# A part kept in SBUF until the merge: when a PSUM bank comes free in a cross-network kernel on one core

## The chip, the cores and the metric

The kernel runs on one core of a Trainium2 chip. The time is that of the device for one execution, in microseconds; lower is better. The kernel before was run three times: median 1504.7 us (1504.6, 1504.7 and 1512.56).

## The reference

For each of 1024 rows, 39 embeddings of 16 numbers are fetched and go through three layers of products (a compressed interaction network), and the results through a small MLP:

```python
x0 = xk = inputs                      # (1024, 39, 16)
for W in (f0, f1, f2):                # W: (F*G, 128)
    z = einsum('bfd,bgd->bfgd', x0, xk).reshape(b, f * g, d)
    cur = einsum('bpd,pm->bmd', z, W) # (1024, 128, 16)
    outs.append(cur); xk = cur
result = sum(concatenate(outs, axis=1), axis=-1)      # (1024, 384)
h = concatenate([result, dense_ctx], axis=1)
h = maximum(h @ W_top1 + b_top1, 0); h = maximum(h @ W_top2 + b_top2, 0); y = h @ W_top3
```

All data is fp32.

## The kernel before

The rows are worked in 8 batch tiles of 128 rows. Each batch tile is four groups (q = 0 to 3), each group four tiles (j = 0 to 3) of 128 columns (8 rows by 16 dimensions). There are 128 tiles in all, numbered t.

The second layer (f1) is where the time goes. For each tile, TensorE multiplies the first layer's result cur0 with f1 for all 39 fields, four fields at a time: that is a **chunk**, c = 0 to 9, of 512 columns in one PSUM bank (chunk 9 has three fields, 384 columns). A chunk is three matmuls, since the product is split in high and low parts: L738, L739, L740. The 39 products of a tile are then each scaled by their field's x and summed. Two ways of doing this share the work:

- chunks 0 and 1, 4 and 5, 8 and 9 (units 0, 2, 4; a **unit** is two banks): ScalarE scales each field in place (L465), then VectorE adds the unit's eight fields in one reduce: L610 for unit 0 (step **R0**, it starts sum_a), L619 for unit 2 (step **R1**, it writes the **part**), L630 for unit 4 (step **R2**, it gives the tile's result, cur1).
- chunks 2, 3, 6 and 7: VectorE multiplies and adds field by field (L605; the first into sum_b is L596), alternately into sum_a and sum_b. These are the steps from FUSE2, FUSE3, FUSE6 and FUSE7 on.

After R1 the part is added to sum_a (L621, **JOIN**). The last but one field of chunk 7 leaves sum_b plus itself in its own bank (LAST_B). The **MERGE** (L627) adds sum_a to that and puts it into the free fourth slot of chunk 9's bank, where the last reduce takes it in.

Every engine runs its instructions in the order in which they are written; semaphores tie the engines together. VectorE counts its 21 steps a tile on the semaphore acc_steps. Y is a ring of three units, six banks: chunk c of a tile goes to the bank that was used three units earlier, and TensorE waits for the step in the table FREED that sets this bank free (L727 to L730). So chunk 9 goes where chunk 3 was, chunks 0 and 1 of the next tile where 4 and 5 were (R1), chunk 2 where 6 was, chunk 3 where 7 was (MERGE), chunk 4 where 8 was (R2).

Between the chunks TensorE has other matmuls at fixed places: the first layer's sums of the next group (L686, seven a group: before chunks 2, 5 and 8 of j=1, chunks 1, 4 and 7 of j=2, chunk 0 of j=3), the product that spreads a tile's cur1 (L694, before chunk 5), transposes of the next batch tile's rows (before chunk 2 where q=2), the transposes of the scalars (L673, before chunk 9 of j=3), the third layer of the batch tile before (L700, before chunks 0 to 3 of j=0 where q is 1 to 3), and the MLP (L708 to L724, in the first tile of q=0 from batch tile 2 on, and in tile 125). In j=3 VectorE also splits the next group's cur0 (L572) and sums it (L574) right before R1. GpSimd gathers the rows and multiplies the pairs for the first layer.

In batch tile 0 and in q=0 of batch tile 1 there is neither third layer nor MLP; these are called plain groups below.

Of the kernel before, what the change touches and what calls it, by code (L numbers as in the profile page):

```python
# [8 lines left out]
ALU = mybir.AluOpType  # L9
ACT = mybir.ActivationFunctionType  # L10
AX = mybir.AxisListType

P = 128
B, NF, D = 1024, 39, 16
M = 128
# [30 lines left out]
SUM_SLOT = 3  # L46


R0, FUSE2, FUSE3, R1, JOIN, FUSE6, FUSE7, MERGE, R2 = 1, 2, 6, 10, 11, 12, 16, 20, 21
NST = 21  # L50

LAST_B = (7, 2)
FREED = {0: R0, 1: R0, 2: FUSE2 + 3, 3: JOIN, 4: R1, 5: R1, 6: FUSE6 + 3, 7: MERGE, 8: R2, 9: R2}


SLOTS = JT * CH
# [75 lines left out]
def build(nc, dense, ids, tables, w1, b1, w2, b2, w3, f0, f1, f2, out):  # L132
    ctx = ExitStack()
    with ctx:
        def sb(name, shape, dt=F32):
            return ctx.enter_context(nc.sbuf_tensor(name, shape, dt))
# [4 lines left out]
        def sem(name):  # L141
            return ctx.enter_context(nc.semaphore(name))
# [26 lines left out]
        x_col = sb("x_col", [P, QG, JT, FC])  # L169
        sum_a = sb("sum_a", [P, 2, M])  # L170
        sum_b = sb("sum_b", [P, 2, M])
        cur1 = sb("cur1", [P, 2, M])

        x_block = sb("x_block", [P, 2, JT, TB * FC])
# [30 lines left out]
        y_filled, scaled, acc_steps = sem("y_filled"), sem("scaled"), sem("acc_steps")  # L205
# [29 lines left out]
        def bank(t, c):  # L235
            b = 2 * ((UNITS * t + c // 2) % UB) + c % 2
            return Y[:, 512 * b:512 * (b + 1)]

        def unit(t, u):
            b = 2 * ((UNITS * t + u) % UB)  # L240
            return Y[:, 512 * b:512 * (b + 2)].rearrange("p (s m) -> p m s", m=M)
# [287 lines left out]
        def _(dve):  # L529
# [40 lines left out]
            def split_cur0(g):  # L570
                dve.wait_ge(cur0_high_ready, g + 1)
                dve.tensor_tensor(cur0_low[:, g % 2, :], C[:], cur0_high[:, g % 2, :].bitcast(F32),  # L572
                                  ALU.subtract).then_inc(cur0_ready, 1)
                dve.tensor_reduce(z0[:, GB * g % (3 * P):GB * g % (3 * P) + GB],  # L574
                                  C[:].rearrange("p (b d) -> p b d", d=D), AX.X, ALU.add).then_inc(c_read, 1)

            def layer2_read(bt, part):
                z = z2[:]
                dve.wait_ge(l2_filled, L2_PARTS * bt + part + 1)
                if part == 0:  # L580
                    dve.tensor_copy(z, C[:, 0:P]).then_inc(c_read, 1)
                else:
                    dve.wait_ge(c_read, C_USE["l2", bt, part])
                    dve.tensor_tensor(z, C[:, 0:P], z, ALU.add).then_inc(c_read, 1)

            def fuse(t, c, first, starts):

                n0 = NST * t
                q, j = t // JT % QG, t % JT
                dve.wait_ge(y_filled, CH * t + c + 1)  # L590
                for i, f in enumerate(CH_F[c]):
                    acc = (sum_a, sum_b)[(i + starts) % 2][:, t % 2, :]
                    src = bank(t, c)[:, i * M:(i + 1) * M]
                    x = x_col[:, q, j, f:f + 1]
                    if c == 2 and i == 1:
                        dve.tensor_scalar(acc, src, x, None, ALU.mult).then_inc(acc_steps, 1)  # L596
                    else:
                        before = first + i - 2
                        if c == 2 and i == 0:
                            before = R0  # L600
                        if c == 6:
                            before = (FUSE3 + 3, JOIN)[i] if i < 2 else before
                        dve.wait_ge(acc_steps, n0 + before)
                        to = src if (c, i) == LAST_B else acc
                        dve.scalar_tensor_tensor(to, src, x, acc, ALU.mult, ALU.add).then_inc(acc_steps, 1)  # L605

            def tile(t, g, q, j):
                n0 = NST * t
                dve.wait_ge(scaled, NSC * t + 2)
                dve.tensor_reduce(sum_a[:, t % 2, :], unit(t, 0), AX.X, ALU.add).then_inc(acc_steps, 1)  # L610
                fuse(t, 2, FUSE2, 0)
                fuse(t, 3, FUSE3, 0)
                if j == 0 and q and g >= QG:
                    layer2_read(g // QG - 1, q - 1)
                if j == JT - 1 and g + 1 < NG:
                    split_cur0(g + 1)
                dve.wait_ge(scaled, NSC * t + 4)
                part = bank(t, 3)[:, 0:M]
                dve.tensor_reduce(part, unit(t, 2), AX.X, ALU.add).then_inc(acc_steps, 1)  # L619
                dve.wait_ge(acc_steps, n0 + R1)  # L620
                dve.tensor_tensor(sum_a[:, t % 2, :], part, sum_a[:, t % 2, :], ALU.add).then_inc(acc_steps, 1)  # L621
                fuse(t, 6, FUSE6, 1)
                fuse(t, 7, FUSE7, 1)
                dve.wait_ge(scaled, NSC * t + 6)
                dve.wait_ge(acc_steps, n0 + FUSE7 + 3)
                c, i = LAST_B
                dve.tensor_tensor(bank(t, 9)[:, SUM_SLOT * M:], bank(t, c)[:, i * M:(i + 1) * M], sum_a[:, t % 2, :],  # L627
                                  ALU.add).then_inc(acc_steps, 1)
                dve.wait_ge(acc_steps, n0 + MERGE)
                dve.tensor_reduce(cur1[:, t % 2, :], unit(t, 4), AX.X, ALU.add).then_inc(acc_steps, 1)  # L630

            split_cur0(0)
            for g in range(NG):
                for j in range(JT):
                    tile(JT * g + j, g, g % QG, j)
# [4 lines left out]
        def _(pe):  # L640
# [86 lines left out]
            def chunk(t, c):  # L727
                v = UNITS * t + c // 2 - UB
                if v >= 0 and (c % 2 == 0 or v % UNITS not in SCALED_UNITS):
                    pe.wait_ge(acc_steps, NST * (v // UNITS) + FREED[2 * (v % UNITS) + c % 2])  # L730
                g, j = divmod(t, JT)
# [121 lines left out]
```

## Time and profile before

| | |
|---|---|
| median of 3 runs | 1504.7 us |
| the profiled execution | 1519.59 us |
| its span | 1517.5 us |
| TensorE matmul busy (PE) | 1363.7 us, 90% |
| VectorE busy (DVE) | 1140.5 us, 75% |
| ScalarE busy (ACT) | 912.2 us, 60% |
| GpSimd busy (POOL) | 702.5 us, 46% |
| granted TensorE clock, mean over the span | 0.954 |

The span is what the profiler saw on the core; the execution's own time is 2.1 us more. PE is the matmul side of TensorE and PEld its weight loads; matmuls are pipelined, so the printed duration of one (some 400 ns) is longer than the distance to the next (0.23 us). In the timeline, an idle time stands in brackets with the instruction that ended it. The granted clock is 1.00 at 2.4 GHz and 0.50 at 1.2 GHz; a window's figure is the mean over it.

### The profile page before, as it was taken

What the parts mean: (1) busy time and instruction counts of PE and PEld (TensorE: products, weight loads), DVE (VectorE), ACT (ScalarE), POOL (GpSimd) and SP (SyncE); (2) the same over time, 40 slices, a digit from 0 to 9 for tenths busy, and PEclk for the clock granted to TensorE, in tenths of its full rate; (3) what the DMA queues carried; (4) which work ended last, traced back from release to release, by engine and by line L of the source; (5) the groups of instructions that cost most, each with busy time, mean ns of one, the idle gap of its engine ahead of it and who ended that gap; (6) DMA issues with size and microseconds to landing.
All of it is one profiled execution on the core that took longest, in us unless ns stands there. A gap on an engine that the chain in (4) does not pass through costs nothing.

```text
span 1517.5 us, 20072 instructions
## 1 busy us (share of the span) xinstructions
PE 1363.7 (90%) x5856; PEld 1021.7 (67%) x5856; DVE 1140.5 (75%) x2792; ACT 912.2 (60%) x3233; POOL 702.5 (46%) x697
## 2 busy tenths in 40 slices
PE   0288999999999999999999999999999999999998
PEld 0166666776767776677777677777767777767677
DVE  0368888888878886878868878687887888687874
ACT  1146666666656665656656666466666666566564
POOL 6676555455634455544535546254564422233200
PEclk8599999999999998999989999899999999899999
DMA  4261021101210021100201002010211102110000
GB/s 96 65 184 29 12 77 40 39 25 37 67 39 27 12 64 45 41 29 2 83 26 46 25 9 88 27 35 23 57 53 32 38 1 69 36 43 24 1 1 1
DMA packets 51355, 62.47 MB, mean 41 GB/s; under 512 B 12707, under 2 KB 24725, under 8 KB 51245
## 3 DMA queue, kind: packets, MB, share of 16 engines
q1 hardware_dynamic: 33644, 54.64, 11.7%
q0 software_dynamic: 10128, 2.98, 1.9%
q10 hardware_dynamic: 7473, 3.56, 1.0%
q8 instruction: 47, 0.77, 0.2%
q14 instruction: 63, 0.52, 0.1%
HBM read 10.02 MB, written 0.00 MB: 7 GB/s over the span
## 4 chain that ended last, share of the span: by engine, by line
PE 69%; DVE 17%; ACT 8%; issue 3%; ACTq 2%; DMA 1%; DVEq 0%
PE Y L738 15%; PE Y L740 14%; PE Y L739 14%; PE C L686 13%; ACT Y L465 8%; PE C L700 5%; DVE Y L619 5%; PE S L694 3%; DVE sum_a L610 3%; DVE sum_a L605 3%; ACTq L233 1%; DVE sum_b L605 1%; DVE sum_a L621 1%; DVE z L574 1%; DVE cur_low L572 1%
## 5 line engine op out<-in xcount | busy, mean ns | idle before, releaser
L465 ACT ACTIVATE Y<-Y,x_col 128x128 f32<-128x128 f32 x2944 | 805.1, 349 | 517.4 <-PE Y L740 469.8
L738 PE MATMUL Y<-f_high,cur_high 128*128 128x512 f32 (+1 forms) x1280 | 641.2, 501 | 88.1 <-DVE sum_a L621 81.4
L367 POOL TENSOR_TENSOR pairs<-shifted,base 117x512 f32<-117x512 f32 x186 | 240.3, 1294 | 586.4 <-PE C L686 584.5
L740 PE MATMUL Y<-f_high,cur_low 128*128 128x512 f32 (+1 forms) x1280 | 504.8, 394 | 0.0
L739 PE MATMUL Y<-f_low,cur_high 128*128 128x512 f32 (+1 forms) x1280 | 504.7, 394 | 0.0
L738 PEld LDWEIGHTS Y<-f_high,cur_high 128*128 128x128 f32 x1280 | 246.0, 192 | 218.0 <-DVE sum_a L621 115.2
L605 DVE SCALAR_TENSOR_TENSOR sum_a<-Y,x_col,sum_a 128x128 f32<-128x128 f32 x1024 | 350.9, 343 | 13.9 <-DVE sum_a L610 0.5
L329 POOL DMA_INDIRECT rows<-in_tbl_dram,ids_sb x312 | 304.8, 977 | 80.4 <-issue 63.3
L739 PEld LDWEIGHTS Y<-f_low,cur_high 128*128 128x128 f32 x1280 | 246.9, 193 | 89.9 <-issue 52.2
L740 PEld LDWEIGHTS Y<-f_high,cur_low 128*128 128x128 f32 x1280 | 244.9, 191 | 52.6
L610 DVE TENSOR_REDUCE sum_a<-Y 128x128 f32<-128x1024 f32 x128 | 156.8, 1225 | 151.2 <-ACT Y L465 147.2
L605 DVE SCALAR_TENSOR_TENSOR sum_b<-Y,x_col,sum_b 128x128 f32<-128x128 f32 x768 | 262.4, 342 | 0.5 <-DVE sum_a L605 0.4
L686 PE MATMUL C<-pairs,f_sum 117*128 117x512 f32 (+1 forms) x448 | 230.2, 596 | 5.7 <-DVE pairs L568 5.6
L619 DVE TENSOR_REDUCE Y<-Y 128x128 f32<-128x1024 f32 x128 | 157.4, 1230 | 100.8 <-ACT Y L465 88.5
L630 DVE TENSOR_REDUCE cur<-Y 128x128 f32<-128x1024 f32 x128 | 156.7, 1224 | 4.4
L686 PEld LDWEIGHTS C<-pairs,f_sum 117*128 117x128 f32 (+1 forms) x448 | 83.9, 191 | 28.8 <-issue 9.8
L700 PEld LDWEIGHTS C<-G,f_sb 128*128 128x128 f32 x624 | 92.4, 211 | 7.7 <-issue 1.1
L700 PE MATMUL C<-G,f_sb 128*128 128x128 f32 x624 | 93.5, 296 | 0.6 <-ACT G L457 0.6
L694 PE MATMUL S<-x_block,cur 128*128 128x320 f32 x256 | 89.7, 432 | 0.0
L351 POOL TENSOR_TENSOR x_block<-x_col,block 128x320 f32<-128x320 f32 x128 | 88.4, 726 | 0.3
L367 POOL TENSOR_TENSOR pairs<-x_seq,base 117x512 f32<-117x512 f32 x31 | 39.7, 1279 | 54.2 <-DMA base<-x_seq 54.2
L457 ACT ACTIVATE G<-S 128x320 f32<-128x320 f32 x128 | 58.3, 456 | 3.1 <-PE S L694 3.1
(77 smaller groups left out, 613.2 us busy)
## 6 DMA issues: line engine op xcount, KB each, us to landing
shifted<-x_seq SPq DMA_DIRECT2D x157, 234.0 KB
base<-x_seq SPq DMA_DIRECT2D x95, 78.0 KB
rows<-in_tbl_dram,ids_sb POOLq DMA_INDIRECT x312
shifted<-x_seq SPq DMA_DIRECT2D x31, 156.0 KB
G<-in_L_rec_f_dram ACTq DMA_DIRECT2D x3, 832.0 KB, 8.8
w_sb<-in_W_top_dram SPq DMA_DIRECT2D x1, 768.0 KB
w_sb<-in_W_top_dram SPq DMA_DIRECT2D x1, 512.0 KB
shifted<-x_seq ACTq DMA_DIRECT2D x2, 234.0 KB
```

The lines of the kernel that those rows point to most:

```text
L329: pool.indirect_dma_start(out=rows[:, f * D:(f + 1) * D], out_offset=None, in_=tables[f], in_offset=bass.IndirectOffsetOnAxis(ap=ids_sb[:, ...
L367: pool.tensor_tensor(pairs[0:r, z % RING, :], shift, base[0:r, g % 2, :], ALU.mult)\
L465: ins = act.activation(where[:, i * M:(i + 1) * M], where[:, i * M:(i + 1) * M], ACT.Copy, scale=x_col[:, t // JT % QG, t % JT, f:f + 1])
L605: dve.scalar_tensor_tensor(to, src, x, acc, ALU.mult, ALU.add).then_inc(acc_steps, 1)
L610: dve.tensor_reduce(sum_a[:, t % 2, :], unit(t, 0), AX.X, ALU.add).then_inc(acc_steps, 1)
L619: dve.tensor_reduce(part, unit(t, 2), AX.X, ALU.add).then_inc(acc_steps, 1)
L630: dve.tensor_reduce(cur1[:, t % 2, :], unit(t, 4), AX.X, ALU.add).then_inc(acc_steps, 1)
L686: pe.matmul(C[:], f0_sum[0:r, k, :], pairs[0:r, z % RING, :], start=k == 0, stop=k == K0 - 1).then_inc(cur0_summed, 1)
L700: ins = pe.matmul(C[:, 0:P], f2_sb[:, f, :], half[:, f, :], start=f == first, stop=f == end - 1)
L738: pe.matmul(where, ch, wh, start=True, stop=False)
L739: pe.matmul(where, ch, wl, start=False, stop=False)
L740: pe.matmul(where, cl, wh, start=False, stop=True).then_inc(y_filled, 1)
```

## The change

The part gets an SBUF tensor of its own, double-buffered like sum_a. R1 writes into it. The fields of chunks 6 and 7 that went into sum_a go into the part instead; sum_a is complete after chunk 3. The join moves behind chunk 7 and adds sum_a to the bank with sum_b, in place; the merge then adds the part. The bank of chunk 3 is given as free with chunk 3's last field (FUSE3 + 3, step 9) instead of with the join (step 11). The number of steps and of instructions is the same.

```diff
@@ -46,11 +46,12 @@
 SUM_SLOT = 3


-R0, FUSE2, FUSE3, R1, JOIN, FUSE6, FUSE7, MERGE, R2 = 1, 2, 6, 10, 11, 12, 16, 20, 21
+R0, FUSE2, FUSE3, R1, FUSE6, FUSE7, JOIN, MERGE, R2 = 1, 2, 6, 10, 11, 15, 19, 20, 21
 NST = 21

+
 LAST_B = (7, 2)
-FREED = {0: R0, 1: R0, 2: FUSE2 + 3, 3: JOIN, 4: R1, 5: R1, 6: FUSE6 + 3, 7: MERGE, 8: R2, 9: R2}
+FREED = {0: R0, 1: R0, 2: FUSE2 + 3, 3: FUSE3 + 3, 4: R1, 5: R1, 6: FUSE6 + 3, 7: MERGE, 8: R2, 9: R2}


 SLOTS = JT * CH
@@ -169,6 +170,7 @@
         x_col = sb("x_col", [P, QG, JT, FC])
         sum_a = sb("sum_a", [P, 2, M])
         sum_b = sb("sum_b", [P, 2, M])
+        part = sb("part", [P, 2, M])
         cur1 = sb("cur1", [P, 2, M])

         x_block = sb("x_block", [P, 2, JT, TB * FC])
@@ -589,7 +591,7 @@
                 q, j = t // JT % QG, t % JT
                 dve.wait_ge(y_filled, CH * t + c + 1)
                 for i, f in enumerate(CH_F[c]):
-                    acc = (sum_a, sum_b)[(i + starts) % 2][:, t % 2, :]
+                    acc = (sum_a if c < 4 else part, sum_b)[(i + starts) % 2][:, t % 2, :]
                     src = bank(t, c)[:, i * M:(i + 1) * M]
                     x = x_col[:, q, j, f:f + 1]
                     if c == 2 and i == 1:
@@ -599,7 +601,7 @@
                         if c == 2 and i == 0:
                             before = R0
                         if c == 6:
-                            before = (FUSE3 + 3, JOIN)[i] if i < 2 else before
+                            before = (FUSE3 + 3, R1)[i] if i < 2 else before
                         dve.wait_ge(acc_steps, n0 + before)
                         to = src if (c, i) == LAST_B else acc
                         dve.scalar_tensor_tensor(to, src, x, acc, ALU.mult, ALU.add).then_inc(acc_steps, 1)
@@ -615,17 +617,17 @@
                 if j == JT - 1 and g + 1 < NG:
                     split_cur0(g + 1)
                 dve.wait_ge(scaled, NSC * t + 4)
-                part = bank(t, 3)[:, 0:M]
-                dve.tensor_reduce(part, unit(t, 2), AX.X, ALU.add).then_inc(acc_steps, 1)
-                dve.wait_ge(acc_steps, n0 + R1)
-                dve.tensor_tensor(sum_a[:, t % 2, :], part, sum_a[:, t % 2, :], ALU.add).then_inc(acc_steps, 1)
+                dve.tensor_reduce(part[:, t % 2, :], unit(t, 2), AX.X, ALU.add).then_inc(acc_steps, 1)
                 fuse(t, 6, FUSE6, 1)
                 fuse(t, 7, FUSE7, 1)
+                c, i = LAST_B
+                b_and_a = bank(t, c)[:, i * M:(i + 1) * M]
+                dve.wait_ge(acc_steps, n0 + FUSE7 + 2)
+                dve.tensor_tensor(b_and_a, b_and_a, sum_a[:, t % 2, :], ALU.add).then_inc(acc_steps, 1)
                 dve.wait_ge(scaled, NSC * t + 6)
-                dve.wait_ge(acc_steps, n0 + FUSE7 + 3)
-                c, i = LAST_B
-                dve.tensor_tensor(bank(t, 9)[:, SUM_SLOT * M:], bank(t, c)[:, i * M:(i + 1) * M], sum_a[:, t % 2, :],
-                                  ALU.add).then_inc(acc_steps, 1)
+                dve.wait_ge(acc_steps, n0 + JOIN)
+                dve.tensor_tensor(bank(t, 9)[:, SUM_SLOT * M:], b_and_a, part[:, t % 2, :], ALU.add)\
+                   .then_inc(acc_steps, 1)
                 dve.wait_ge(acc_steps, n0 + MERGE)
                 dve.tensor_reduce(cur1[:, t % 2, :], unit(t, 4), AX.X, ALU.add).then_inc(acc_steps, 1)

```

No instruction of TensorE, ScalarE, GpSimd or SyncE moves. On VectorE, in every tile: the rows from R1 on, in the kernel before (line, operation, out<-in, what it waits for):

```order
L619 TENSOR_REDUCE Y<-Y 128x128 [waits scaled]
L621 TENSOR_TENSOR sum_a<-Y,sum_a 128x128 [waits acc_steps]
L605 SCALAR_TENSOR_TENSOR sum_b<-Y,x_col,sum_b 128x128 [waits acc_steps,y_filled]
L605 SCALAR_TENSOR_TENSOR sum_a<-Y,x_col,sum_a 128x128 [waits acc_steps]
L605 SCALAR_TENSOR_TENSOR sum_b<-Y,x_col,sum_b 128x128 [waits acc_steps]
L605 SCALAR_TENSOR_TENSOR sum_a<-Y,x_col,sum_a 128x128 [waits acc_steps]
```

and with the change (R1 is L620 there, a field L607):

```order
L620 TENSOR_REDUCE part<-Y 128x128 [waits scaled]
L607 SCALAR_TENSOR_TENSOR sum_b<-Y,x_col,sum_b 128x128 [waits acc_steps,y_filled]
L607 SCALAR_TENSOR_TENSOR part<-Y,x_col,part 128x128 [waits acc_steps]
L607 SCALAR_TENSOR_TENSOR sum_b<-Y,x_col,sum_b 128x128 [waits acc_steps]
L607 SCALAR_TENSOR_TENSOR part<-Y,x_col,part 128x128 [waits acc_steps]
L607 SCALAR_TENSOR_TENSOR sum_b<-Y,x_col,sum_b 128x128 [waits acc_steps,y_filled]
```

The join between the reduce and chunk 6 is gone, and the fields run into part. The end of the tile on VectorE before, from the third field of chunk 7 to the last reduce:

```order
L605 SCALAR_TENSOR_TENSOR sum_a<-Y,x_col,sum_a 128x128 [waits acc_steps]
L605 SCALAR_TENSOR_TENSOR Y<-Y,x_col,sum_b 128x128 [waits acc_steps]
L605 SCALAR_TENSOR_TENSOR sum_a<-Y,x_col,sum_a 128x128 [waits acc_steps]
L627 TENSOR_TENSOR Y<-Y,sum_a 128x128 [waits acc_steps,scaled]
L630 TENSOR_REDUCE cur<-Y 128x128 [waits acc_steps]
```

and with the change, from the same place:

```order
L607 SCALAR_TENSOR_TENSOR part<-Y,x_col,part 128x128 [waits acc_steps]
L607 SCALAR_TENSOR_TENSOR Y<-Y,x_col,sum_b 128x128 [waits acc_steps]
L607 SCALAR_TENSOR_TENSOR part<-Y,x_col,part 128x128 [waits acc_steps]
L626 TENSOR_TENSOR Y<-Y,sum_a 128x128 [waits acc_steps]
L629 TENSOR_TENSOR Y<-Y,part 128x128 [waits acc_steps,scaled]
L632 TENSOR_REDUCE cur<-Y 128x128 [waits acc_steps]
```

The join (L626) stands between the last field and the merge (L629), and waits for the field before the last; the wait for ScalarE's last scaling (scaled) is still the merge's.

## Rows read from the trace of the kernel before

**Rows 1.** The page, part 1: busy us, share of span, instructions.

```profile
PE 1363.7 (90%) x5856; PEld 1021.7 (67%) x5856; DVE 1140.5 (75%) x2792; ACT 912.2 (60%) x3233; POOL 702.5 (46%) x697
```

**Rows 2.** Waits: engine, line, for whom; us in total, times, longest.

```profile
PE Y L738 <- DVE sum_a L621: 81.4, 59, 2.3
...
DVE Y L619 <- ACT Y L465: 88.5, 77, 3.1
```

**Rows 3.** Groups by line and shape: count, busy us, mean ns, idle before.

```profile
L619 DVE TENSOR_REDUCE Y<-Y 128x128 f32<-128x1024 f32 x128 | 157.4, 1230 | 100.8 <-ACT Y L465 88.5 <-issue 12.3
L610 DVE TENSOR_REDUCE sum_a<-Y 128x128 f32<-128x1024 f32 x128 | 156.8, 1225 | 151.2 <-ACT Y L465 147.2 <-issue 1.1
...
L738 PE MATMUL Y<-f_high,cur_high 128*128 128x384 f32 x128 | 56.8, 444 | 82.2 <-DVE sum_a L621 81.4
```

**Rows 4.** Timeline, end of tile 68 (j=0, q=1), start of 69: start, us, instruction.

```profile
835.22 1.23 DVE L619 TENSOR_REDUCE Y<-Y 128x128 f32<-128x1024 f32 x1 [0.97 <-ACT Y L465]
...
835.74 0.39 PE L740 MATMUL Y<-f_high,cur_low 128*128 128x512 f32 x1
...
836.49 0.29 DVE L621 TENSOR_TENSOR sum_a<-Y,sum_a 128x128 f32<-128x128 f32 x1
...
836.70 0.34 DVE L605 SCALAR_TENSOR_TENSOR sum_b<-Y,x_col,sum_b 128x128 f32<-128x128 f32 x1
...
836.83 0.44 PE L738 MATMUL Y<-f_high,cur_high 128*128 128x384 f32 x1 [0.70 <-DVE sum_a L621]
...
837.47 0.40 PE L738 MATMUL Y<-f_high,cur_high 128*128 128x512 f32 x1
...
838.51 0.34 DVE L605 SCALAR_TENSOR_TENSOR sum_a<-Y,x_col,sum_a 128x128 f32<-128x128 f32 x1
...
838.95 0.30 DVE L627 TENSOR_TENSOR Y<-Y,sum_a 128x128 f32<-128x128 f32 x1
...
839.28 1.22 DVE L630 TENSOR_REDUCE cur<-Y 128x128 f32<-128x1024 f32 x1
...
840.41 0.40 PE L738 MATMUL Y<-f_high,cur_high 128*128 128x512 f32 x1
...
841.11 0.39 PE L738 MATMUL Y<-f_high,cur_high 128*128 128x512 f32 x1
```

**Rows 5.** Timeline, end of group: tile 71 (j=3, q=1) and start of 72.

```profile
866.03 1.22 DVE L619 TENSOR_REDUCE Y<-Y 128x128 f32<-128x1024 f32 x1
...
867.64 0.44 PE L738 MATMUL Y<-f_high,cur_high 128*128 128x384 f32 x1 [2.03 <-DVE sum_a L621]
...
869.08 0.77 PE L738 MATMUL Y<-f_high,cur_high 128*128 128x512 f32 x1
```

**Rows 6.** Timeline, TensorE: chunk 9 of tile 75 (j=3, q=2), of MLP tile 96.

```profile
912.57 0.44 PE L738 MATMUL Y<-f_high,cur_high 128*128 128x384 f32 x1 [1.59 <-DVE sum_a L621]
...
1150.76 0.60 PE L724 MATMUL C<-h,w_sb 128*1 128x128 f32 x4
1151.48 0.45 PE L738 MATMUL Y<-f_high,cur_high 128*128 128x384 f32 x1
```

**Rows 7.** Timeline, weight load of chunk 4 of tile 12 (j=0, plain group).

```profile
211.33 0.19 PEld L738 LDWEIGHTS Y<-f_high,cur_high 128*128 128x128 f32 x1 [0.57 <-DVE cur L630]
```

**Rows 8.** Windows: length, busy us of each engine (count), PEclk, DMA share, GB/s.

```profile
100.00:1495.00 1395.00, 1311.59 (x5614) 983.13 (x5613) 1110.99 (x2733) 887.25 (x3169) 631.68 (x618) 0.97 0.13 36
865.00:870.00 5.00, 2.97 (x19) 2.62 (x18) 4.86 (x13) 2.19 (x8) 0.00 (x0) 0.91 0.00 0
1138.94:1152.11 13.17, 12.88 (x71) 9.86 (x70) 6.17 (x15) 7.42 (x27) 0.00 (x0) 1.00 0.01 2
960.18:976.66 16.48, 16.36 (x71) 12.53 (x71) 5.59 (x14) 7.49 (x27) 0.00 (x0) 0.76 0.01 1
510.32:521.13 10.81, 10.11 (x57) 8.42 (x56) 8.17 (x21) 6.97 (x24) 0.00 (x0) 1.00 0.01 2
333.19:345.60 12.41, 11.71 (x58) 9.80 (x56) 7.88 (x20) 6.96 (x24) 0.00 (x0) 0.86 0.00 1
```

The last four are from the first matmul of chunk 0 of a tile to that of the next: the MLP tiles 96 and 80, and the tiles 40 and 24 (both j=0, q=2).

## The prediction

> **What bounds the kernel now.** I read the page's first two parts, then the waits of TensorE, then the timeline of one group of four tiles, then the granted clock in windows. The page shows TensorE busy for 90% of the span and VectorE for 75% [rows 1], so the question is what TensorE waits for. The waits answer it with one line: it sits idle 81.4 us in 59 places before a matmul of L738, each time released by L621, the join of the part into sum_a [rows 2]. Grouped by shape, practically all of it stands before the 384-wide L738, which is chunk 9 alone [rows 3]. Chunk 9 goes into the bank that held chunk 3, and that bank holds the part until the join has read it.
>
> The 59 places are of two kinds. In tiles with j=0 the idle time is 0.70 us [rows 4]; there are 26 such tiles, and the two last tiles of the program are alike. At the end of each group (j=3, 31 times) it is 2.03 us [rows 5], or 1.59 us where the tile also carries a transpose, q=2 [rows 6], because VectorE splits cur0 (two instructions, L572 and L574) just before the reduce. 28 x 0.70 + 24 x 2.03 + 7 x 1.59 = 79.5 us, so the two kinds are the whole wait. In tiles j=1 and j=2 the join ends just as TensorE arrives, and nothing is lost.
>
> There is a second cost behind the first. The granted clock between 100 and 1495 us is 0.97 on average, which is 2 x 0.03 x 1395 = 84 us at the lower of the two levels (1.2 GHz) [rows 8]. Between 865 and 870 us one sees how it begins: TensorE busy 2.97 of 5 us (the 2.03 us idle), then the clock falls, 0.91 in that window. I looked at every fall between 100 us and the tail: 15 of them, each beginning at most 4 us after an end-of-group idle of 1.6 to 2.0 us began, none elsewhere (16 such idles had no fall behind them).
>
> **The change, part by part.** *The wait.* Chunk 9 now waits for the last field of chunk 3 (step FUSE3+3), which VectorE finishes before it even starts the reduce. So chunk 9 never waits. But chunk 0 of the next tile goes into a bank of chunks 4 and 5, and still waits for the reduce R1. That is what comes late next, so I follow each stall to it.
>
> *j=0 tiles, q=1 and 3.* Reduce ends at 835.22+1.23 = 836.45, a semaphore takes 0.05 (L621 ends 836.78, L738 starts 836.83), so chunk 0 may start at 836.50 [rows 4]. TensorE would run chunk 9 at 835.97 (its L740 of chunk 8 starts 0.23 earlier than that), 0.86 earlier than now, and be at chunk 0 at 837.47-0.86 = 836.61: no wait. Chunk 3 comes at 840.41-0.86 = 839.55; its bank is free with the merge, 839.25+0.05: no wait. Chunk 4 comes at 841.11-0.86 = 840.25, but its bank waits for R2, which ends at 839.28+1.22 = 840.50: it starts at 840.57. Of the 0.86, 0.33 goes back and 0.53 stays. Tiles j=1 and j=2 are set by TensorE's own work, so the 0.53 is carried on. With q=2 the transpose before chunk 2 covers the wait for R2 and the whole 0.86 stays.
>
> *Ends of groups.* Chunk 9 starts 2.03 earlier. The next tile begins with third-layer matmuls and then chunk 0, which waits for R1: 866.03+1.22+0.05 = 867.30 instead of the 869.08 of now, a gain of 1.78; TensorE itself would be there at 867.05, so 0.25 of the 2.03 remains as a wait [rows 5]. With q=2 all of 1.59 is gained [rows 6]. Before an MLP tile (q=0, batch tiles 2 to 7) some 3 us of other matmuls stand ahead of chunk 0, so all 2.03 is gained.
>
> *The MLP tiles and the plain groups.* In an MLP tile chunk 9 waits little: L738 starts 0.72 after the first of four small matmuls of L724 that take 0.60 [rows 6]; I take 0.2, between 0 and 0.86. In batch tile 0 and the first group of batch tile 1 there is no third layer; TensorE already waits 0.57 for R2 there [rows 7], VectorE's chain from R1 to R2 to R1 sets the pace, and the ends of groups give nothing; I take 0.5 a group, between 0 and 1.
>
> *The sum.* Ends: 15 x 1.78 + 6 x 1.59 + 6 x 2.03 = 48.4. j=0: 15 x 0.53 + 6 x 0.86 + 6 x 0.2 + 5 x 0.5 = 16.8. Together 65 us. (The last batch tile has no transposes, so its q=2 counts with q=1 and 3; one of the seven groups with transposes is plain.)
>
> *VectorE's own work.* It issues as many instructions a tile as before. The reduce writes to SBUF instead of PSUM: between the 1225 ns of L610 and the 1230 of L619 [rows 3], no change. The old join cost 0.21 of the chain (836.49 to 836.70) and that goes. The new join stands after the last field: 0.26 if it only queues, 0.44 if it must wait as L627 does behind L605 (838.51 to 838.95), and the merge behind it 0.33 (as L630 behind L627) in place of the 0.44 of today [rows 4]. So R2 moves by 0.26+0.33-0.44-0.21 = -0.06 to +0.12 us; I take 0.02. It only counts where chunk 4 waits for R2 (some 20 groups): at most 2 us. The semaphore waits of the join hold nobody else, since VectorE has only its own fields behind it. ScalarE is idle before most chunks it scales and gets chunk 9 earlier.
>
> *The clock.* What a fall costs is seen in twin stretches: an MLP tile takes 13.17 us at a clock of 1.00 and 16.48 at 0.76, a tile j=0 of q=2 10.81 against 12.41 at 0.86 [rows 8]. That is 3.31 us for 2 x 0.24 x 16.48 = 7.9 us at the low level, and 1.60 for 3.5, so 0.42 to 0.46 a microsecond; 84 x 0.42 = 35 us. If the idle time of 2 us is what lets the clock fall, a remainder of 0.25 should not, and 35 us go too. The MLP tile at 1.00 shows that small matmuls alone don't bring it down.
>
> In this trace the idles of 0.70 us were never followed by a fall without one of 1.6 to 2.0 us, so I take the 35 us as gained. A rule of the Trainium skill speaks against that, in "TensorE: Matmul & The Clock Gate", section "A second HAM failure mode: psum-queue depth-cycling": a kernel that cycles its matmuls through PSUM banks idles for very short times between groups, and that alone can keep the clock swinging. This kernel cycles six banks. By that rule the gain would be 65 us and not 100; its case is rival (a).
>
> **From the profile to the median.** The profiled execution took 1519.6 us (its span 1517.5 and 2.1 around it, which stay), the median is 1504.7, and the three runs lie 8 us apart, which is the size of a few falls of the clock. If the 15 us are falls that the profile had and the median didn't, both end at 1519.6-65-35 = 1420; if the profile itself costs 15, the median ends at 1405. I take 1417, nearer the first.
>
> **Rivals.**
> (a) The clock still falls, by micro-idles or by the MLP's small matmuls. For it: the longest low stretches lie in MLP tiles. Against it: an MLP tile at 1.00. Time 1504.7-65 = 1440.
> (b) The stall only moves: chunk 0 and chunk 4 wait for R1 and R2 more than I computed, because VectorE (75% busy) slips late in every tile; then about half the 65 stays and part of the falls too: 1504.7-33-15 = 1457. For it: R2 is already what chunk 4 meets after a j=0 tile. Against it: VectorE idles 88.5 us in 77 places before L619, waiting for ScalarE [rows 2], so it has time to spare in most tiles.
> (c) The waits are hidden anyway or the bank isn't free earlier in effect: no change, 1500 to 1512. Against it: a released wait of 81 us on an engine busy 90%.
> (d) Slower. Mechanism: with the idle time spread in pieces of 0.3 us over all groups, TensorE's clock spends much more time at the low level. Price 0.42 us each; it has to eat the 65 us and leave none of the 35, so it decides from 84+65/0.42 = 239 us at the low level, 17% of the span; then 1510 and more. Against it: nothing of the sort follows the 0.70 idles now.
>
> **The numbers.** Forecast (wait and clock both gone) 0.66, with its own range 1398 to 1432; (a) 0.15; (b) 0.11; (c) 0.05; (d) 0.03. The time is the likeliest case's, 1417. The range 1400 to 1450 holds the forecast nearly whole and (a), and leaves out (b) to (d) and the lower tip. A difference of 0.5% (7.5 us) is about what a measurement of this kernel can tell from no change. Faster is the forecast, (a) and (b) and a little of (c): 0.93; same 0.04; slower 0.03.
>
> **What would show it.** In the changed profile the wait of L738 for the join is gone, and no idle stands before the 384-wide matmul. New waits appear before the 512-wide ones: about 0.25 us on the reduce at 15 ends of groups, about 0.3 on R2's reduce after j=0 tiles with q=1 and 3, more in the plain groups; all of them under 20 us. Busy VectorE time stays at 1140 us. The clock between 100 us and the end is 0.99 or 1.00. I am wrong on the clock if it is still 0.97 with the waits gone, and wrong on the sum if waits on R1 and R2 exceed 30 us.

## The result, and the profile after

The changed kernel takes 1398.3 us (median of 4 runs, 1397.7 to 1401.9) against 1504.7 us of the kernel before (4 runs, 1503.4 to 1512.6). The ratio is 0.929, with a 95% interval of 0.926 to 0.932. It is 106 us faster; 88 us were forecast (1417).

The page of the changed kernel, its busy times, the granted clock in 40 slices and the costliest TensorE group (line, operation, count, busy us, mean ns, idle before it):

```profile
span 1396.1 us, 20072 instructions
...
PE 1320.1 (95%) x5856; PEld 992.7 (71%) x5856; DVE 1125.4 (81%) x2792; ACT 908.1 (65%) x3233; POOL 703.1 (50%) x697
...
PEclk8599999999999999999999999999999999999998
...
L740 PE MATMUL Y<-f_high,cur_high 128*128 128x512 f32 (+1 forms) x1280 | 627.7, 490 | 9.3 <-DVE part L620 4.6
```

TensorE is now busy 95% of the span, with the same 5856 matmuls as before [rows 1]. The waits of the matmuls and of the weight loads for VectorE, in two lists (us in total, times, longest):

```profile
PE Y L740 <- DVE part L620: 4.6, 5, 1.2
...
PE Y L740 <- DVE cur L632: 1.7, 6, 0.3
```

```profile
PEld Y L740 <- DVE cur L632: 12.4, 24, 0.7
...
PEld Y L740 <- DVE sum_b L607: 7.5, 31, 0.2
...
PEld Y L740 <- DVE part L620: 6.1, 33, 0.5
```

The 81.4 us for the join [rows 2] have no successor. What is left are waits for R1 (part) and R2 (cur), a few microseconds in the matmuls and somewhat more in the weight loads. Nearly all of the 4.6 us for R1 stand before chunk 0 of tiles 4, 8, 12 and 16, behind ends of plain groups. The longest of them:

```profile
233.21 0.47 PE L740 MATMUL Y<-f_high,cur_high 128*128 128x512 f32 x1 [1.22 <-DVE part L620]
```

By shape, the chunk 9 matmul and two of the three reduces (columns as in [rows 3]):

```profile
L620 DVE TENSOR_REDUCE part<-Y 128x128 f32<-128x1024 f32 x128 | 156.4, 1222 | 83.8 <-ACT Y L467 83.6
L612 DVE TENSOR_REDUCE sum_a<-Y 128x128 f32<-128x1024 f32 x128 | 156.2, 1221 | 64.9 <-ACT Y L467 64.2
...
L740 PE MATMUL Y<-f_high,cur_high 128*128 128x384 f32 x128 | 46.4, 363 | 0.0
```

No idle stands before the 384-wide matmul, and its own duration fell from 444 to 363 ns. The place of [rows 4] in the changed kernel, the end of tile 68 and the start of tile 69:

```profile
770.04 1.23 DVE L620 TENSOR_REDUCE part<-Y 128x128 f32<-128x1024 f32 x1 [0.69 <-ACT Y L467]
...
770.55 0.40 PE L742 MATMUL Y<-f_high,cur_low 128*128 128x512 f32 x1
...
770.79 0.34 PE L740 MATMUL Y<-f_high,cur_high 128*128 128x384 f32 x1
770.97 0.34 PE L741 MATMUL Y<-f_low,cur_high 128*128 128x384 f32 x1
...
771.18 0.34 DVE L607 SCALAR_TENSOR_TENSOR sum_b<-Y,x_col,sum_b 128x128 f32<-128x128 f32 x1
...
771.32 0.50 PE L740 MATMUL Y<-f_high,cur_high 128*128 128x512 f32 x1
...
772.99 0.34 DVE L607 SCALAR_TENSOR_TENSOR part<-Y,x_col,part 128x128 f32<-128x128 f32 x1
...
773.24 0.29 DVE L626 TENSOR_TENSOR Y<-Y,sum_a 128x128 f32<-128x128 f32 x1
...
773.64 0.30 DVE L629 TENSOR_TENSOR Y<-Y,part 128x128 f32<-128x128 f32 x1
...
773.97 1.22 DVE L632 TENSOR_REDUCE cur<-Y 128x128 f32<-128x1024 f32 x1
...
775.25 0.19 PEld L740 LDWEIGHTS Y<-f_high,cur_high 128*128 128x128 f32 x1 [0.44 <-DVE cur L632]
775.25 0.50 PE L740 MATMUL Y<-f_high,cur_high 128*128 128x512 f32 x1
```

Chunk 9 starts 0.24 us after the start of chunk 8's last matmul (770.55), long before the reduce R1 ends (771.27). Chunk 0 of the next tile starts just behind R1 (771.32), and chunk 4 (775.25) just behind R2 (775.19), as the prediction had it. The place of [rows 5] (end of a group), TensorE and the reduce:

```profile
799.44 0.42 PE L740 MATMUL Y<-f_high,cur_high 128*128 128x384 f32 x1
...
800.07 1.22 DVE L620 TENSOR_REDUCE part<-Y 128x128 f32<-128x1024 f32 x1
...
800.30 1.13 PE L702 MATMUL C<-G,f_sb 128*128 128x128 f32 x8
...
801.34 0.50 PE L740 MATMUL Y<-f_high,cur_high 128*128 128x512 f32 x1
```

The 2.03 us are gone; the third layer's matmuls fill the time until R1 ends (801.29), and chunk 0 starts then. The window over the steady part (columns as in [rows 8]):

```profile
100.00:1370.00 1270.00, 1259.32 (x5582) 947.73 (x5581) 1087.20 (x2715) 876.52 (x3146) 626.70 (x613) 1.00 0.14 39
```

The clock is 1.00. Between 100 us and the tail it doesn't fall once, not even behind the idles of 1.2 us at the plain ends; before, it fell 15 times there and stayed at the lower level for 85 us. (In the first 20 us of the tiles it is at the lower level for 0 to 6 us in each profile, in both kernels; falls are counted from 100 us to the tail here and below.)

Where the span's 121.4 us went (1517.5 - 1396.1), by the stretch from the first matmul of chunk 0 of tile 0 to the first of chunk 9 of tile 127, called the **loop** below: 119.1 us in the loop (1413.1 to 1293.9), 4.3 in the start before it, and 2.0 the other way in the tail. The start isn't the change's: it lasted between 77.9 and 90.6 us in the profiles of this study, in both kernels. The experiments below split the loop's 119 us.

### The profile page after: what moved, and what is told of

It is laid out like the page before. It is cut to its first block, busy times and chain, and to the rows that moved or that the text cites. A ratio compares the mean times of both kernels' runs of the same rounds, so it can differ in the third digit from the quotient of the medians.

```text
span 1396.1 us, 20072 instructions
## 1 busy us (share of the span) xinstructions
PE 1320.1 (95%) x5856; PEld 992.7 (71%) x5856; DVE 1125.4 (81%) x2792; ACT 908.1 (65%) x3233; POOL 703.1 (50%) x697
## 3 DMA queue, kind: packets, MB, share of 16 engines
q1 hardware_dynamic: 33644, 54.64, 12.7%
HBM read 10.02 MB, written 0.00 MB: 7 GB/s over the span
## 4 chain that ended last, share of the span: by engine, by line
PE 88%; DVE 4%; POOL 3%; ACT 2%; issue 2%; DMA 1%; SPq 0%; DVEq 0%
PE Y L740 20%; PE Y L742 19%; PE Y L741 19%; PE C L688 14%; PE C L702 5%; PE S L696 5%; POOL rows L331 3%; ACT Y L467 2%; PE C L720 1%; PE C L710 1%; PE C L711 1%; PE S L662 1%; DVE sum_b L607 1%; ACT h L474 1%; DVE sum_a L612 1%
## 5 line engine op out<-in xcount | busy, mean ns | idle before, releaser
L740 PE MATMUL Y<-f_high,cur_high 128*128 128x512 f32 (+1 forms) x1280 | 627.7, 490 | 9.3 <-DVE part L620 4.6
L742 PE MATMUL Y<-f_high,cur_low 128*128 128x512 f32 (+1 forms) x1280 | 498.3, 389 | 0.0
L741 PE MATMUL Y<-f_low,cur_high 128*128 128x512 f32 (+1 forms) x1280 | 497.6, 389 | 0.0
L369 POOL TENSOR_TENSOR pairs<-shifted,base 117x512 f32<-117x512 f32 x186 | 240.3, 1294 | 471.5 <-PE C L688 469.6
L740 PEld LDWEIGHTS Y<-f_high,cur_high 128*128 128x128 f32 x1280 | 241.0, 188 | 122.9 <-issue 46.3
L741 PEld LDWEIGHTS Y<-f_low,cur_high 128*128 128x128 f32 x1280 | 242.1, 189 | 92.3 <-issue 52.2
L607 DVE SCALAR_TENSOR_TENSOR sum_b<-Y,x_col,sum_b 128x128 f32<-128x128 f32 x768 | 262.6, 342 | 0.0
L620 DVE TENSOR_REDUCE part<-Y 128x128 f32<-128x1024 f32 x128 | 156.4, 1222 | 83.8 <-ACT Y L467 83.6
L607 DVE SCALAR_TENSOR_TENSOR sum_a<-Y,x_col,sum_a 128x128 f32<-128x128 f32 x512 | 176.1, 344 | 13.9 <-PE Y L742 0.5
L607 DVE SCALAR_TENSOR_TENSOR part<-Y,x_col,part 128x128 f32<-128x128 f32 x512 | 175.1, 342 | 0.0
L702 PEld LDWEIGHTS C<-G,f_sb 128*128 128x128 f32 x624 | 82.8, 194 | 13.1 <-issue 6.8
L702 PE MATMUL C<-G,f_sb 128*128 128x128 f32 x624 | 85.9, 279 | 2.2 <-ACT G L459 0.6
L369 POOL TENSOR_TENSOR pairs<-x_seq,base 117x512 f32<-117x512 f32 x31 | 39.8, 1283 | 52.5 <-DMA base<-x_seq 52.5
```

The lines of the kernel that those rows point to most:

```text
L369: pool.tensor_tensor(pairs[0:r, z % RING, :], shift, base[0:r, g % 2, :], ALU.mult)\
L702: ins = pe.matmul(C[:, 0:P], f2_sb[:, f, :], half[:, f, :], start=f == first, stop=f == end - 1)
L740: pe.matmul(where, ch, wh, start=True, stop=False)
L741: pe.matmul(where, ch, wl, start=False, stop=False)
L742: pe.matmul(where, cl, wh, start=False, stop=True).then_inc(y_filled, 1)
```

## The experiments

The theory: chunk 9's wait made two costs that add up, the stalls (some 80 us) and the falls of the clock that the long ones of them bring (some 40 us). Rivals: part of the gain comes from the new order on VectorE; the clock was slow for another reason. A second question is why the stalls were worth 15 us more than the sum: did the tiles j=1 and 2 lose something after all, or did the places that were counted lose more than their printed idle? The expectations on record name their theories themselves.

These runs were made on other chips than the first result; the kernel before takes 1513 to 1515 us there, 8 to 11 more. The late gates ran on one (1515.4), the run with the sharper gate on another (1512.9), all others on a third (1513.3), with both kernels once more among them. Every ratio is to the kernel before on the same chip, and the ratios are to be compared, not the medians: the expectations name times of the first chip. The loop differs little between chips (changed kernel 1293.9 and 1294.6 us).

### All of it undone by the one number

The new order on VectorE stays, only chunk 9 waits as late as before (for the first field after R1). The next three experiments have another tuple at the same place.

```diff
-                    pe.wait_ge(acc_steps, NST * (v // UNITS) + FREED[2 * (v % UNITS) + c % 2])
+                    free = FREED[2 * (v % UNITS) + c % 2]
+                    if c == 9 and t % JT in (0, 1, 2, 3):
+                        free = FUSE6
+                    pe.wait_ge(acc_steps, NST * (v // UNITS) + free)
```

> The changed kernel, but chunk 9 waits in every tile for the first field of chunk 6 (FUSE6, step 11), which ends 0.38 us after the reduce R1; the old join ended 0.33 us after it. So the late release is back and the new layout of the sums stays. Theory A (all of the 106 us is TensorE's wait for the bank, with what the wait costs in exposed weight loads and in falls of the clock): 1500 to 1512 us, within a few us of the kernel before. Theory B (a good part comes from VectorE's shorter chain, part in SBUF and no join behind R1): clearly below, 1480 or less.

Measured: 1503.3 us, ratio 0.991 (0.987 to 0.994). Its matmul wait and its window:

```profile
PE Y L743 <- DVE sum_b L607: 76.9, 59, 2.2
```

```profile
100.00:1370.00 1270.00, 1198.06 (x5164) 899.54 (x5163) 1013.63 (x2519) 816.63 (x2922) 615.45 (x602) 0.97 0.14 40
```

The wait is back at 59 places, the clock falls 13 times, and nearly the whole time is back. So the gain is the wait's, not the new order's. 12 us stay away (1515.4 to 1503.3), more than the few that were expected; they fit the gate: the first field ends 0.25 us behind R1 (0.38 was expected), the old join 0.33, and in tiles without a fall each kind is shorter than before by 0.07 to 0.09, which makes some 10 us in 127 tiles.

### The tiles of one kind alone

```diff
+                    if c == 9 and t % JT in (1, 2):
```

The second run has (0,) in the place of (1, 2), the third (3,).

> The same late release, but only in the tiles j=1 and j=2, where the kernel before showed practically no idle time before chunk 9 (0.00 to 0.02 us), because the join ended just as TensorE arrived. Theory A1 (a wait that ends just in time still costs about 0.1 us, since the weight load of the waiting matmul can't be done ahead of it: 0.64 us from chunk 9 to chunk 0 before, 0.52 after): 64 x 0.1 to 0.15 = 6 to 10 us over the changed kernel, 1404 to 1408. Theory A2 (only printed idle time costs): 1398 to 1401.

> The late release only in the tiles j=0. The idle of 0.7 us before chunk 9 comes back there, and the wait of chunk 4 for R2 in the next tile goes away. Theory A: 15 x 0.67 + 6 x 1.0 + 6 x 0.25 + 5 x 0.7 = about 21 us more, 1415 to 1422, and the granted clock stays at 1.00 between 100 us and the tail, since idles of 0.7 us bring no fall. Rival (short idles let the clock fall as well): falls appear, and the time is 1425 or more.

> The late release only in the tiles j=3. The idle of 2.0 us at the end of each group comes back, 27 x 1.8 = 49 us. Theory A with the clock (the 2 us idle is what lets the clock fall): falls are back in the trace, mean clock between 100 us and the tail 0.97 to 0.98, and another 20 to 30 us: 1465 to 1478. Rival (the falls came of something else): clock 1.00, 1445 to 1450. With e2 and e3 the sum of the three losses should be that of e1.

The changed kernel itself, run with the kernels of the next sections:

> The changed kernel again, unchanged, beside the kernel before on the same chip as the other runs of this set: a base for them. Both theories: ratio 0.929 as in the first comparison; no fall of the clock between the first tile and the tail; and the time from chunk 0 of tile 0 to chunk 9 of tile 127 is 1294 us, whatever the time before it (gathers and loads) is on this chip.

| late in | median us | ratio (interval) | loop us, first row in full | falls, us at 1.2 GHz |
|---|---|---|---|---|
| none (third chip) | 1407.6 | 0.930 (0.926 to 0.934) | 1294.6 | 0 |
| j=1, 2 | 1412.9 | 0.932 (0.929 to 0.936) | +4.8 | 0 |
| j=0 | 1425.9 | 0.941 (0.937 to 0.944) | +20.2 | 0 |
| j=3 | 1498.9 | 0.987 (0.983 to 0.992) | +91.0 | 13, 99 |
| all | 1503.3 | 0.991 (0.987 to 0.994) | +100.7 | 13, 68 |

Waits and windows of the j=0 and the j=3 kernel:

```profile
PE Y L743 <- DVE sum_b L607: 16.7, 26, 1.0
```

```profile
100.00:1370.00 1270.00, 1242.24 (x5485) 934.34 (x5484) 1076.28 (x2680) 866.30 (x3101) 634.44 (x620) 1.00 0.14 40
```

```profile
PE Y L743 <- DVE sum_b L607: 57.4, 32, 2.2
```

```profile
100.00:1370.00 1270.00, 1214.69 (x5182) 919.14 (x5181) 1015.48 (x2532) 817.70 (x2932) 616.98 (x603) 0.96 0.14 40
```

The changed kernel came out as expected in ratio and loop (0.929 and 1294). With 26 idles of 0.64 us on average, 1.0 at most, in the j=0 tiles the clock stays at 1.00; with the idles at the ends of groups it falls. Only those ends cost clock. They cost more than expected (91 us, where 67 to 80 were): this kernel spent 99 us at the low level, and the expectation took 20 to 30 us for it. At 0.43 each the 99 are some 43 us; the 48 that remain are the stall, as expected (49). The j=0 tiles cost the 20 us that their own stall was expected to; that their median of 1425.9 stands in the rival's range (1425 or more) is the chip's doing, since the ratio 0.941 is 1415 us on the first, and no fall is there. The three losses alone make 116 us, more than the 101 with all gates late, since that kernel had 31 us less at the low level (13 us of time). The run with j=1 and 2 late came out at +5 where some 6 to 10 were expected, and only 2.5 of the 5 stand from tile 16 on. It doesn't decide: its gate is itself 0.08 us earlier than the old join. It is sharpened below.

### The clock alone: other work in the idle time

The kernel before again, and the kernel before with 16 matmuls of 192 columns, whose results nobody reads, put before chunk 9 at the ends of groups (30 of the 31).

```diff
+FILL = 16
...
+                        for n in range(FILL):
+                            pe.matmul(S[:, 320:512], cur0_high[:, g % 2, 0:P],
+                                      f1_high[:, 2 * n:2 * n + 2, :].rearrange("p f m -> p (f m)")[:, 0:192],
+                                      start=True, stop=True)
```

> The kernel before again, with a profile of its own. If its spread between runs comes from how many falls of the clock it catches and from the time before the first tile, then the stretch from chunk 0 of tile 0 to chunk 9 of tile 127, less 0.43 us for each us at the low level, is 1377 us again (1413.1 less 36.7 in the first profile). If something else varies, it is not.

> The kernel before, with 16 extra matmuls (192 columns, into a part of bank S that nobody reads) behind the transposes of the scalars in j=3, that is in the 2.03 us in which TensorE waits there. They leave the wait as long as it is and only fill it with work. Clock theory (it is the idle time that lets the clock fall): no falls after the first tile, and 1377 to 1382 us from chunk 0 of tile 0 to chunk 9 of tile 127, 25 to 36 us less than before by the median. Rival (the MLP's and third layer's small matmuls or the many short idles bring the falls): falls stay, time within 5 us of the kernel before.

Measured: 1516.1 us for the kernel before (against its other runs on that chip a ratio of 1.001, 0.999 to 1.003, which says how good the comparison is) and 1486.0 with the filling, ratio 0.981 (0.978 to 0.985). The waits and windows, first of the kernel before on this chip, then of the filled one:

```profile
PE Y L738 <- DVE sum_a L621: 81.1, 59, 2.3
```

```profile
100.00:1370.00 1270.00, 1194.38 (x5129) 896.02 (x5128) 1015.90 (x2498) 811.60 (x2897) 611.85 (x599) 0.97 0.14 39
```

```profile
PE Y L739 <- DVE sum_a L622: 29.1, 52, 2.3
```

```profile
100.00:1370.00 1270.00, 1244.02 (x5704) 941.68 (x5704) 1040.65 (x2563) 833.20 (x2969) 625.58 (x610) 1.00 0.14 40
```

The 480 matmuls more make the kernel 27 us faster than the median of the kernel before on that chip (1513.3), and 30 faster than its run beside it. They let nothing start earlier: chunk 9 still waits for the join, only with 0.23 us of idle instead of 2.03 (with q=2 none; the 0.70 in the j=0 tiles stay, and one of 2.3 in the last batch tile, where no filling stands). A tile in which the clock stays up is as long as in the kernel before (10.41 us with j=0, 11.12 at an end of group, in both). The clock doesn't fall any more. This separates the two costs: the loop takes 1374.3 us with every stall and no fall, against 1413.1 and 1404.7 in the two profiles of the kernel before, with 85.3 and 71.7 us at the low level. That is 38.8/85.3 = 0.455 and 30.4/71.7 = 0.424 us for each, inside the 0.42 to 0.46 that the prediction read from twin stretches. The rest, 1374.3 - 1294.3 (the two profiles of the changed kernel), is 80 us of stall, and 80 + 39 are the loop's 119. Two expectations came out somewhat low. The filled loop of 1374.3 lies under the 1377 to 1382 named. And at 0.43 each the second profile of the kernel before gives 1404.7 - 30.8 = 1373.9 without falls, where 1377 again was expected, so the price isn't known better than to some 3 us of the whole.

### Lost time that is not printed as idle

The sharpened run: chunk 9 one field later still (R1's end plus about 0.5 us), in j=1 and 2 only.

```diff
                     if c == 9 and t % JT in (1, 2):
-                        free = FUSE6
+                        free = FUSE6 + 1
```

The edit is shown against the kernel with j=1 and 2 late.

> As the kernel with the late release in j=1 and j=2 (0.04 us a tile lost there), but chunk 9 waits for the second field of chunk 6, which ends 0.26 us later. If a wait costs the time by which it ends after the point where the weight load could have begun (about 0.1 us before the matmul), then each of these 64 tiles loses 0.04+0.26 = 0.30 us, 19 us in all, less what the next wait for R2 gives back after j=1 tiles (nothing there) and j=0 (none); the printed idle before chunk 9 is only about 0.15 us in each. From chunk 0 of tile 16 to chunk 9 of tile 127: 1138.6+17 = 1155 to 1157 us. If only printed idle counts: 1138.6+9 = 1148 us.

Measured: 1426.0 us, ratio 0.942 (0.936 to 0.947; kernel before: 1512.9 there), and a loop 19.6 us longer than the changed kernel's on the third chip; from tile 16 on it takes 1154.9 us (the changed kernel 1138.6), where 1155 to 1157 was expected if a wait costs more than its printed idle, and 1148 if it costs its idle. Its row of chunk 9 shows almost no idle, 3.4 us in all:

```profile
L743 PE MATMUL Y<-f_high,cur_high 128*128 128x384 f32 x128 | 53.1, 415 | 3.4 <-DVE part L607 1.6
```

The timeline of chunk 9 of tile 69 (j=1) there:

```profile
799.46 0.40 PE L745 MATMUL Y<-f_high,cur_low 128*128 128x512 f32 x1
...
799.87 0.19 PEld L743 LDWEIGHTS Y<-f_high,cur_high 128*128 128x128 f32 x1 [0.46 <-DVE part L607]
799.88 0.44 PE L743 MATMUL Y<-f_high,cur_high 128*128 128x384 f32 x1
...
800.15 0.34 PE L744 MATMUL Y<-f_low,cur_high 128*128 128x384 f32 x1
```

Two losses are visible and neither is printed. L745 starts at 799.46 and a free L743 would start 0.23 later, at 799.69; it starts at 799.88, but since L745 is drawn 0.40 long, the list sees no idle. And the weight load waited with its matmul: it starts at 799.87 instead of beside the matmul before, so the next matmul comes 0.27 behind instead of the 0.18 of a free chunk 9 (770.79 to 770.97 above). 0.19 + 0.09 = 0.28 us, and the tiles of j=1 and j=2 got longer by 0.28 and 0.31.

### A version that is faster than both

In a group's second tile (j=1) chunk 4 waits for R2, while a first-layer sum stands before chunk 5. It is put before chunk 4 instead.

```diff
-AT_SUM = [12 + 3 * k for k in range(K0)]
+AT_SUM = [12, 14] + [12 + 3 * k for k in range(2, K0)]
```

> The changed kernel with one of the seven first-layer sums a group moved from before chunk 5 to before chunk 4 in j=1, so that it fills the wait of chunk 4 for R2. In 20 tiles that wait is 0.17 us and its exposed weight load 0.11: 4 to 6 us less than the changed kernel if such a just-in-time wait costs what I think; 0 to 3 us less if only the idle part counts.

Measured: 1402.1 us (1400.5 to 1403.6) against 1407.6 (1405.1 to 1409.9) of the changed kernel on the same chip; ratio to the kernel before 0.926 (0.922 to 0.929), against 0.930. The place in tile 69 (chunk 4 of j=1), to be read against 773.97 to 775.25 above:

```profile
781.72 1.22 DVE L632 TENSOR_REDUCE cur<-Y 128x128 f32<-128x1024 f32 x1
...
782.83 1.02 PE L688 MATMUL C<-pairs,f_sum 117*128 117x512 f32 x2
...
783.26 0.19 PEld L740 LDWEIGHTS Y<-f_high,cur_high 128*128 128x128 f32 x1 [0.24 <-issue]
783.29 0.79 PE L740 MATMUL Y<-f_high,cur_high 128*128 128x512 f32 x1
```

The sum runs while R2 does (782.83, R2 ends at 782.94), and chunk 4 doesn't wait for R2 any more. A j=1 tile (q=1, 3) takes 10.01 us instead of 10.32, and from tile 16 on the loop is 5.3 us shorter, where 4 to 6 were expected if a wait that ends just in time costs its weight load too, and 0 to 3 if only its idle counts. The four runs of each don't overlap, though 5.5 us is 0.4% and so less than the 0.5% that the prediction held to be clear of no change; the tiles' lengths are the stronger ground.

## Why the prediction was right, and where it was not

**The wait (step "The wait").** Right. Chunk 9 never waits for the bank, and the run with all gates late shows that this alone is the gain.

**What comes late next.** Right in kind and place: chunk 0 meets R1 at the ends of groups and chunk 4 meets R2 after the j=0 tiles. Together these waits stay below the 20 us that were named. The 0.25 us on R1 at 15 ends are not printed, since the third layer's matmuls are drawn over them (to 801.43 above, where chunk 0 starts at 801.34); the printed ones stand in the plain groups (0.8 to 1.2).

**The sum, 65 us.** This is the step that failed: 80 us measured (the loops 1374.3 and 1294.3 of the experiments). By kind of tile, start to start, medians of the filled kernel's profile and of the second one of the changed kernel; q is the tile's own:

| | predicted | measured |
|---|---|---|
| j=0 tile, q=1, 3 | 0.86 earlier | 10.41 to 9.46: 0.95 |
| j=1 tile behind it | 0.33 given back | 10.02 to 10.32: 0.30 |
| j=2 tile | "nothing is lost": 0 | 10.48 to 10.35: 0.13 |
| end of a group, q=0, 1 | 1.78 | 11.12 to 9.35: 1.77 |
| end of a group, q=2 | 1.59 | 11.12 to 9.35: 1.77 |
| end before an MLP tile, q=3 | 2.03 | 12.79 to 10.67: 2.12 |
| MLP tile | 0.2 | 13.17 to 13.00: 0.18 |
| plain group | 0.5 | 39.8 to 38.6: 1.2 |

The 14 us that were missing come from four places (totals over the tiles of a kind, outside the plain groups and in them):

| | predicted | measured |
|---|---|---|
| the five plain groups, the last one's end at 1.78 | 4.3 | 9.1 |
| all other j=2 | 0 | 4.5 |
| all other j=0 and j=1 | 14.3 | 17.7 |
| all other ends | 46.6 | 48.1 |

First, the tiles in which a wait ends just in time. In j=2 "nothing is lost" was 0.13 a tile, and in j=0 the 0.86 were 0.95. The run with the later gate in j=1 and 2 shows the reason, the weight load that a waiting matmul can't have done ahead (some 0.1 us). It shows too that the drawn length of the matmul before hides up to 0.16 us of idle; in j=0 the prediction had allowed for that, by taking 0.86 from the starts for the 0.70 printed. Both were to be read in the rows of before: chunk 9's L738 is drawn 0.44 long in [rows 4] and 0.45 in the MLP tile where it starts without printed idle [rows 6], against 0.34 of a free one (770.79 above). Second, the plain groups. The fourth one (tiles 12 to 15, without a fall in any of these profiles) takes 38.61 us in the changed kernel, 38.68 with j=1 and 2 late, 38.93 with j=3, 39.11 with j=0, 39.50 with all, and 39.81 in the filled kernel. So j=0 is worth the 0.5 that was taken for the whole group, the ends 0.3 where "the ends of groups give nothing", the middle tiles 0.1, and the 0.3 that stay away with all gates late are the gate's 0.08 a tile. The ends were right to 0.01 us with q=0 and 1, where R1 sets the time on both sides; with q=2 the tile has the same lengths, so R1 sets it there too, and the printed 1.59 was not the measure.

**VectorE's chain.** R1's end to R2's end took 4.05 us before (836.45 to 840.50) and takes 3.92 now (771.27 to 775.19): -0.13, where -0.06 to +0.12 was predicted and +0.02 taken. The fields now start 0.09 before the reduce's printed end (771.18 and 771.27; 0.08 in all 128 tiles); the old join, which needs that result, started 0.04 behind it. So the join's removal saved 0.34 of the chain, not its 0.21. It also explains the busy time: 1140 was predicted to stay and 1125.4 was measured, though the durations of the operations are unchanged (289 ns for the join, 300 for the merge; added one by one they make 1311 us in both kernels). The busy time counts overlapping stretches once, and 128 x 0.12 us more of them overlap now.

**The clock, 35 us.** Right: 39 and 30 us in the two profiles of the kernel before, at 0.424 to 0.455 for each microsecond at the low level. That the long idles are what lets it fall, and the short ones not, was read from coincidence in the trace; the filled kernel and the runs with j=0 and j=3 show it. The prediction's "1.6 to 2.0 us" was too wide: all 15 falls of that trace stand behind idles of 2.0 us, none behind one of 1.59 (q=2). Rival (a) is out: the changed kernel still cycles the six banks with short waits, and between 100 us and the tail its clock doesn't fall once. The rule of the Trainium skill that spoke for it ("TensorE: Matmul & The Clock Gate", section "A second HAM failure mode: psum-queue depth-cycling") isn't borne out by this trace.

**From the profile to the median.** The two ends were 1420 (the 15 us are falls of that one execution, so profile and median end at the same time) and 1405 (the profile itself costs 15), and the forecast took 1417. The 15 us were that execution's own, as the first end had it, whether falls or not: the kernel before's profile lies 14.9 us above its median, but the changed one's at it (1398.1 against 1398.3), and so does the kernel before's on the third chip (1515.7 against 1516.1). With the measured terms the profile's own time gives 1519.6 - 80 - 39 - 4.3 + 2.0 = 1398.3; the second end would have given 15 less. That 1405 is nearer the measured time than 1417 is luck: it makes up for most of what the sum lacked. A longer start (4.3 us against the changed kernel's) and more time at the low level than the median run (the two profiles differ by 14 us of it, 6 us of time) would fit the 15 us; the unprofiled runs have no trace, so that split stays open. The measured time lies at the lower tip of the forecast's own range (1398 to 1432), which the stated range from 1400 on left out.

**The rivals.** (b) falls: the waits for R1 and R2 are small. (c) falls with the result. (d) doesn't occur; the time at the low level went to nothing.

## What to carry to other kernels

Read a wait's cost from start to start of the matmuls, in the waiting place and in a free one, not from the printed idle: a matmul whose wait ends just in time loses its weight load's head start too (some 0.1 us here), and the drawn end of the one before hides idle (up to 0.16 us). A wait at the end of a long chain of banks can be taken away by asking which step really reads the bank last, and the next gate is then priced by the time its own releaser ends. Where idle times of 2 us stand in front of a matmul, look for falls of the clock behind them before pricing the stall: here they were about a third of the gain, and even useless matmuls in the gap paid.

## What the runs showed that was not expected

- A kernel got 27 us faster by 480 matmuls that nobody reads; they did nothing but fill idle times of 2.03 us down to 0.23.
- Between 100 us and the tail the clock fell only behind printed idles of 1.8 to 2.3 us, 1.8 to 4.6 us after they began (13 to 16 times in each of the four profiles with them). It never fell behind the 28 idles of 1.5 to 1.6 us in the same four profiles (the ends with q=2), the three of 1.2 us in the changed kernel, or the 26 of up to 1.0 us in the kernel with the late gate in j=0. It didn't fall behind every long one, and which ones changed from run to run: 72 and 85 us at the low level in the same kernel.
- 3.4 us of printed idle stood for 16 to 20 us of lost time in the kernel with the later gate.
- On VectorE a scalar_tensor_tensor that follows a reduce and doesn't read its result starts 0.08 us before the reduce's printed end (all 128 tiles); the old join, which read it, started 0.04 behind.
- The start, before the first tile, varied from 77.9 to 90.6 us between profiles of the same start in both kernels, 12.7 us that belong to no change.
